# A language-model layer on one core: the first unit's q, k and v projection worked between token tiles 7 and 13

## The chip, the cores and the metric

The kernel runs on 1 core of one Trainium2 chip. The metric is the device time of one execution in microseconds (us), median over runs.

## The reference

The input is 2 sequences of 1024 token numbers, 2048 tokens in all, with rows of 512 features. The layer has three parts.

```
h   = where(is_hot[id], hot_emb[tok2hot[id]], cold_emb[tok2cold[id]] @ proj_w.T)   # 8000 hot rows of 512, 24000 cold of 128
h  += (softmax(causal(q @ k.T / sqrt(32))) @ v) @ w_out.T     # q, k, v = layernorm(h) @ w_project.T; 16 heads of 32
h  += routed top-2-of-16 experts (silu(x Wg) * (x Wu)) Wd, renormalised, + one shared expert    # x = layernorm(h)
```

## The kernel before

The program runs in stages, one instruction stream per engine, written out by hand and joined by semaphores alone. The order in a stream is the order in the code.

**Tables.** Two tables over all 32000 token numbers are built from the list of hot ids with one-hot matmuls into PSUM bank 0.

**Look-ups.** 128 tokens are one tile, 16 tiles (NT) in all. For each tile, TensorE multiplies the one-hot rows of its tokens with the tables (L1605 to L1613, PSUM banks 4 and 5 in turn), and VectorE picks the wanted column with two fused operations (`look_up`, L1523). After every four tiles `row_numbers` (L1535) turns the sums into row numbers for the gathers. All 16 look-ups come first.

**Token tiles.** For each tile c, GpSimd issues two indirect DMAs, one gathers cold rows (L1419) and one hot rows (L1423); then it takes the inverse standard deviation (`inv_std`, L691) of tile c - LAG - 1, with LAG = 4. TensorE turns the cold rows, multiplies them with the projection (L1631), and turns the normalised rows of tile c - 3 (L1639). ScalarE copies both results out of PSUM (L1460, L1464 into xnT). VectorE adds hot and cold rows and takes the statistics (`embed`, L1548), and one tile later it normalises (`norm`, L1559). SyncE stores each tile of h to HBM (L1370).

**The first projection.** Attention works on 8 units, one for 4 heads of one sequence. A unit needs its q, k and v projections: six pieces (FILLS) through PSUM bank 7, numbered q 0 and 1, k 2 and 3, v 4 and 5, where an even piece covers tokens 0 to 511 of the sequence, so tiles 0 to 3, and an odd one tiles 4 to 7. Units 2 to 8 have theirs worked inside the unit before. The first unit's six pieces go in TensorE's turns 11 to 16 of the tile loop (FILL0 = 11, L1642), one each turn, in the order 0 to 5. q and k are needed as a high part (float32r) and a low part. ScalarE copies the q pieces to the buffer `full` and VectorE the k pieces (`fill_evac`, L455); GpSimd makes from it the high part and then the low part (`split_part`, L427), in its own tile loop.

**Stacks.** `stack` (L394) spreads the two parts over the partitions with 16 DMAs of 128 KB for q and 16 for k, all issued by SyncE. q's come between the stores of h tiles 12 and 13, k's after the last store. The first scores (`first_scores`, L556) wait for all 32, for xnT of all 16 tiles (L1647) and for the v pieces.

**After that** come the 8 units of attention, the output projection and the expert stage; the change doesn't touch them.

Of the kernel before, what the change touches and what calls it, by code (L numbers as in the profile page):

```python
# [11 lines left out]
F32 = mybir.dt.float32  # L12
# [28 lines left out]
LAG = 4  # L41
# [3 lines left out]
FILL0 = NT // BATCH + 3  # L45
# [18 lines left out]
def build(nc, a, out):  # L64
    ctx = ExitStack()
    with ctx:
# [38 lines left out]
        oh_lo = tk("oh_lo", [HOT_P, HOT_C, 256], BF16)  # L105
        row_over_chunk = tk("row_over_chunk", [HOT_P, HOT_C])
# [31 lines left out]
        tk("stack_room", [P, HOT_C * 256 - HOT_C * 2], BF16)  # L138
# [255 lines left out]
        def stack(sp, u, b, sides=(0, 1), first=False):  # L394

            if not first:

                sp.wait_ge(s_S, HEAD + (u - 1) * STEPS)
            for side in sides:
                st = (q_stack, k_stack)[side][b]  # L400

                sp.wait_ge(s_lo, HEAD + 4 * u + 2 * side + 2)
                for r in range(4):
                    low = r % 2 if side == 0 else r // 2
                    src = part_lo if low else part_hi
                    for h in range(GH):
                        sp.dma_start(st[32 * r:32 * r + 32, h, :].bitcast(F32),
                                     src[32 * h:32 * h + 32, side, :].bitcast(F32)).then_inc(s_stack[b], 16)

        def att_sp(sp):  # L410
# [10 lines left out]
            group(GROUPS - 1, True)  # L421

# [54 lines left out]

        def fill_piece(pe, u, b, f, k, loads):

            if k == 0:  # L480

                pe.wait_ge(s_w, loads)
                copied, count = ((s_fdve, 0), (s_fact, 1), (s_fact, 2), (s_fdve, 1), (s_fdve, 2), (s_fact, 3))[f]
                pe.wait_ge(copied, HEAD + 3 * u + count)
            if f < 4:
# [867 lines left out]
        def _(sp):  # L1353
# [14 lines left out]
            for c in range(NT):  # L1368
                sp.wait_ge(s_h, c + 1)
                sp.dma_start(h_dram[c * P:(c + 1) * P, :], hot_vec[c][:, :]).then_inc(s_hst, 16)  # L1370
                if c == NT - LAG:
                    stack(sp, 0, 0, (0,), first=True)
            stack(sp, 0, 0, (1,), first=True)
# [4 lines left out]
        def _(pool):  # L1378
            for s in (s_lo, s_hi):
                pool.sem_inc(s, HEAD)  # L1380
# [49 lines left out]
            for c in range(NT - LAG - 1, NT):  # L1430
                inv_std(pool, c)
                if c < NT - 1:

                    half = c - NT + LAG + 1
                    split_part(pool, 0, 0, half // 2, half % 2, None)
# [4 lines left out]
        def _(act):  # L1440
            for s in (s_E, s_Ca, s_fact, s_ZR):
                act.sem_inc(s, HEAD)
            act.wait_ge(s_const, 9)
# [11 lines left out]
            for c in range(NT + 3):  # L1455
# [10 lines left out]
                if 0 <= c - FILL0 < FILLS:  # L1466
                    fill_evac(act, "act", 0, c - FILL0, 0)
# [4 lines left out]
        def _(dve):  # L1472
            for s in (s_M, s_Cd, s_Zr, s_Z, s_AT, s_fdve):
                dve.sem_inc(s, HEAD)
            step = Chain(dve, s_dve)
# [47 lines left out]
            def look_up(c):  # L1523
# [6 lines left out]
                for part, test, total in ((0, ALU.is_le, below), (1, ALU.is_equal, hot_no)):  # L1530
                    dve.scalar_tensor_tensor(out=prod[:, s, part, :], in0=iota_bf[:, :], scalar=tok_lo[:, c:c + 1],
                                             in1=bank(4 + s)[:, 256 * part:256 * part + 256], op0=test,
# [34 lines left out]
            for k in range(BATCHES):  # L1567
                for c in range(k * PER, (k + 1) * PER):
                    look_up(c)
                row_numbers(k)  # L1570
            for c in range(NT + 1):
                if c < NT:
# [3 lines left out]
                if 0 <= c + 1 - FILL0 < FILLS:  # L1576
                    fill_evac(dve, "dve", 0, c + 1 - FILL0, 0)
# [4 lines left out]
        def _(pe):  # L1582
# [22 lines left out]
            for c in range(NT):  # L1605
                if c >= 2:
                    pe.wait_ge(s_looked, 2 * (c - 1))
                b = bank(4 + c % 2)
# [4 lines left out]
                          skip_group_check=True).then_inc(s_look, 1)  # L1613
            pe.wait_ge(s_proj, 16)
            for c in range(NT + 3):
# [7 lines left out]
                if 1 <= c <= NT:  # L1623
                    t = c - 1
                    pe.wait_ge(s_coldC, t + 1)
                    if t == 1:

                        pe.wait_ge(s_looked, 2 * NT)
# [13 lines left out]
                if 0 <= c - FILL0 < FILLS:  # L1642

                    pe.wait_ge(s_xC, NT // BATCH)
                    for k in range(KC):
                        fill_piece(pe, 0, 0, c - FILL0, k, 16)
# [52 lines left out]
```

## Time and profile before

| | us |
|---|---|
| runs of the kernel before | 1059.1, 1061.99, 1067.91 (median 1061.99) |
| profiled execution, its own time | 1064.05 |
| its span | 1062.3 |
| TensorE busy in the span | 970.4 (91%) |
| VectorE, ScalarE, GpSimd busy | 555.0, 487.5, 299.4 |
| the chain that ended last: TensorE's share | 71% |

In the profile PE is TensorE's matmul, PEld its weight load, DVE is VectorE, ACT ScalarE, POOL GpSimd, SP SyncE; a q behind a name means the DMA instructions that the engine issues. Times in the rows are us from the start of the span.

### The profile page before, as it was taken

What the parts mean: (1) busy time and instruction counts of PE and PEld (TensorE: products, weight loads), DVE (VectorE), ACT (ScalarE), POOL (GpSimd) and SP (SyncE); (2) the same over time, 40 slices, a digit from 0 to 9 for tenths busy, and PEclk for the clock granted to TensorE, in tenths of its full rate; (3) what the DMA queues carried; (4) which work ended last, traced back from release to release, by engine and by line L of the source; (5) the groups of instructions that cost most, each with busy time, mean ns of one, the idle gap of its engine ahead of it and who ended that gap; (6) DMA issues with size and microseconds to landing.
All of it is one profiled execution on the core that took longest, in us unless ns stands there. A gap on an engine that the chain in (4) does not pass through costs nothing.

```text
span 1062.3 us, 20312 instructions
## 1 busy us (share of the span) xinstructions
PE 970.4 (91%) x6623; PEld 650.5 (61%) x6623; DVE 555.0 (52%) x1652; ACT 487.5 (46%) x1163; POOL 299.4 (28%) x320
## 2 busy tenths in 40 slices
PE   6668699999999999999998899899899999799994
PEld 5333468686776868686776687778644444344441
DVE  8875257575666657565667677578511111111110
ACT  7212177777767777777778422211122222222221
POOL 2276120111102020111111046333323643354432
PEclk9689899999999999999999999899999999999997
DMA  6133733250624334240533111711368757955443
GB/s 210 39 94 91 171 81 87 73 111 1 136 56 89 72 81 97 69 105 6 131 124 103 62 70 58 277 51 40 109 206 271 146 86 216 286 96 103 88 70 40
DMA packets 44564, 114.31 MB, mean 108 GB/s; under 512 B 9332, under 2 KB 11380, under 8 KB 42162
## 3 DMA queue, kind: packets, MB, share of 16 engines
q1 hardware_dynamic: 32146, 87.14, 28.7%
q0 software_dynamic: 12320, 25.90, 12.9%
q8 instruction: 57, 0.93, 0.4%
q14 instruction: 41, 0.34, 0.1%
HBM read 53.03 MB, written 25.17 MB: 74 GB/s over the span
## 4 chain that ended last, share of the span: by engine, by line
PE 71%; DVE 7%; issue 7%; DMA 6%; POOL 4%; ACT 3%; SPq 1%; POOLq 0%; ACTq 0%; DVEq 0%
PE psum L1258 11%; PE psum L518 11%; PE psum L488 8%; PE psum L531 7%; PE psum L508 7%; DMA w_dn<-in_wd 6%; PE psum L1339 6%; PE psum L493 5%; PE psum L1202 4%; PE psum L1186 3%; PE psum L1279 2%; PE psum L534 2%; PE psum L1301 1%; POOL hot_all L1423 1%; DVE oh_lo L1498 1%
## 5 line engine op out<-in xcount | busy, mean ns | idle before, releaser
L642 DVE CUSTOM_DVE_ANT_0 psum<-psum,mask_row 128x128 f32<-128x128 f32 (+7 forms) x256 | 194.3, 762 | 58.1 <-PE psum L508 55.7
L600 ACT ACTIVATE probs<-psum,nmax 128x128 f32<-128x128 f32 (+7 forms) x256 | 190.4, 744 | 47.4 <-DVE nmax L642 42.7
L1258 PE MATMUL psum<-attnT,x_T 128*128 x376 | 177.5, 594 | 8.2 <-SPq L748 6.9
L518 PE MATMUL psum<-ident,probs 128*128 128x128 f32 x1152 | 173.9, 276 | 4.7 <-ACT probsT L585 3.2
L508 PE MATMUL psum<-k_stack,q_stack 128*128 128x512 f32 (+2 forms) x384 | 155.5, 460 | 16.9 <-issue 8.8
L518 PEld LDWEIGHTS psum<-ident,probs 128*128 128x128 f32 x1152 | 136.9, 141 | 37.0 <-issue 18.9
L1159 DVE COPY x_T<-psum 128x512 f32<-128x512 f32 x47 | 32.5, 691 | 223.8 <-PE psum L1301 223.8
L585 ACT COPY probsT<-psum 128x512 f32<-128x512 f32 (+3 forms) x256 | 129.1, 504 | 37.8 <-PE psum L518 33.0
L488 PE MATMUL psum<-xnT,w_unit 128*128 128x512 f32 x256 | 130.5, 599 | 0.2 <-ACT full L463 0.2
L435 POOL CAST part_hi<-full 128x512 fp32r<-128x512 f32 x32 | 19.6, 612 | 350.7 <-ACT full L463 246.0
L859 POOL DMA_INDIRECT out<-xnT,slot_out x47 | 74.5, 1584 | 150.9 <-DMA out<-xnT,slot_out 104.6
L1258 PEld LDWEIGHTS psum<-attnT,x_T 128*128 128x128 f32 x376 | 67.2, 190 | 77.0 <-issue 76.9
L508 PEld LDWEIGHTS psum<-k_stack,q_stack 128*128 128x128 f32 x384 | 69.0, 202 | 62.0 <-ACT probs L600 39.3
L1339 PE MATMUL psum<-w_dn,gated_T 128*128 x188 | 88.6, 593 | 1.0 <-ACT gated_T L912 1.0
L531 PE MATMUL psum<-probsT,v_unit 128*32 128x128 f32 x2304 | 76.6, 276 | 0.8 <-ACT probsT L585 0.8
L531 PEld LDWEIGHTS psum<-probsT,v_unit 128*32 128x32 f32 x2304 | 59.2, 110 | 27.0 <-ACT probsT L585 21.7
L657 DVE TENSOR_TENSOR attnT<-psum,z_rows 128x128 f32<-128x128 f32 x64 | 18.7, 292 | 107.5 <-ACT z_rows L607 107.5
L931 ACT ACTIVATE xnT<-psum,slot_w 128x512 f32<-128x512 f32 x47 | 32.3, 687 | 83.3 <-PE psum L1339 83.3
L493 PE MATMUL psum<-w_unit,xnT 128*128 128x128 f32 x512 | 66.7, 275 | 0.3 <-DVE full L467 0.3
L587 DVE COPY probsT<-psum 128x128 f32<-128x128 f32 (+3 forms) x128 | 62.3, 486 | 3.0 <-PE psum L518 1.0
L493 PEld LDWEIGHTS psum<-w_unit,xnT 128*128 128x128 f32 x512 | 61.7, 192 | 0.5 <-issue 0.5
L906 ACT ACTIVATE silu_g<-psum 128x256 f32<-128x256 f32 x63 | 24.1, 383 | 79.9 <-PE psum L1258 63.4
(223 smaller groups left out, 1405.8 us busy)
## 6 DMA issues: line engine op xcount, KB each, us to landing
attnT<-in_wgu SPq DMA_DIRECT2D x16, 1024.0 KB, 5.4
q_stack<-part_hi SPq DMA_DIRECT2D x64, 128.0 KB, 2.4
q_stack<-part_lo SPq DMA_DIRECT2D x64, 128.0 KB, 2.4
k_stack<-part_hi SPq DMA_DIRECT2D x64, 128.0 KB, 2.4
k_stack<-part_lo SPq DMA_DIRECT2D x64, 128.0 KB, 2.4
w_dn<-in_wd SPq DMA_DIRECT2D x16, 512.0 KB, 6.1
out<-acc SPq DMA_DIRECT2D x17, 256.0 KB, 2.3
hot_all<-xn SPq DMA_DIRECT2D x4, 1024.0 KB, 8.0
```

The costliest lines, as they stand in the source:

```text
L488: mm = pe.matmul(bank(7), w_unit[:, k, side * P:(side + 1) * P], xnT[:, k, t0:t0 + 512], start=(k == 0), stop=(k == KC - 1), skip_group_ch ...
L493: mm = pe.matmul(bank(7)[:, k * P:(k + 1) * P], xnT[:, c, t0:t0 + P], w_unit[:, c, 2 * P:3 * P], start=(c == 0), stop=(c == KC - 1))
L508: mm = pe.matmul(dst[:, c0:c1], qs, k_stack[b][:, h, c0:c1], start=True, stop=True)
L518: mm = pe.transpose(bank(4 + m % 2)[:, (j - 4 * k) * P:(j - 4 * k + 1) * P], probs[n % PSLOTS][:, j * P:(j + 1) * P], ident[:, :])
L531: pe.matmul(bank(6)[32 * h:32 * h + 32, 0:P], v_unit[b][:, j, 32 * h:32 * h + 32], probsT[i % 2][:, h, j * P:(j + 1) * P], start=(j == 0), ...
L585: eng.copy(dst, src).then_inc(s_Ca, 1)
L587: eng.tensor_copy(dst, src).then_inc(s_Cd, 1)
L600: act.activation(probs[n % PSLOTS][:, 0:(i + 1) * P], bank(2 * (n % 2), 2)[:, 0:(i + 1) * P], ACT.Exp, bias=nmax[:, n % 4:n % 4 + 1], scal ...
L642: dve.tensor_tensor_reduce(out=row, in0=row, in1=mask_row[:, (QT - 1 - i) * P:QT * P], scale=1.0, scalar=3.0e38, op0=ALU.add, op1=ALU.min, ...
L859: pool.indirect_dma_start(out=out, out_offset=bass.IndirectOffsetOnAxis(ap=slot_out[:, j:j + 1], axis=0), in_=y_rows[j % ROUTED_RING], in_ ...
L1258: mm = pe.matmul(bank(2 + p), lhs(k), rhs(k), start=(k == 0), stop=(k == KC - 1), skip_group_check=True)
L1339: mm = pe.matmul(bank(6 + p), gated_T[:, p, k * P:(k + 1) * P], w_dn[:, bass.ds(half, 1), k, :].rearrange("p o n -> p (o n)"), start=(k == 0),
```

## The change

Six things change, all of them before the first scores.

1. Ten look-ups (`EARLY_LOOKS`) come ahead of the tile loop on TensorE and VectorE; the other six are done in turns 1 to 6 of the loop, one each, with `row_numbers` for tiles 8 to 11 in turn 2 and for 12 to 15 in turn 6. The late odd look-ups use bank 7 (`look_bank`).
2. LAG goes from 4 to 2, so GpSimd takes `inv_std` of tile c - 3 behind the gathers of tile c.
3. The six pieces are worked in TensorE's turns 7, 8, 9, 11, 12 and 13 in the order 0, 2, 4, 1, 3, 5 (`FIRST_FILL`). Piece 0 waits for all look-ups.
4. ScalarE makes the high part straight from bank 7 (`first_high`) and VectorE the low part from bank 7 and the high part (`first_low`), ahead of that turn's `embed`. GpSimd has no part in it any more, and the copies to `full` go.
5. SyncE issues the q stacks behind the store of h tile 10. ScalarE issues the k stacks, 8 DMAs at the end of its turn 13 and 8 at the end of its turn 14.
6. ScalarE, VectorE and SyncE wait for the last store of h before attention. A block of unused room (`stack_room`) moves, so that the q and k stacks lie over memory that is free by then.

```diff
@@ -38,11 +38,12 @@
 WRING = 4
-LAG = 4
+LAG = 2
+EARLY_LOOKS = 10
+FIRST_FILL = {7: 0, 8: 2, 9: 4, 11: 1, 12: 3, 13: 5}
 SPLIT0 = 5
 SLOT0 = 6
-FILL0 = NT // BATCH + 3
 PSLOTS = 2
@@ -103,6 +104,7 @@
         oh_lo = tk("oh_lo", [HOT_P, HOT_C, 256], BF16)
+        tk("stack_room", [P, HOT_C * 256 - HOT_C * 2], BF16)
         row_over_chunk = tk("row_over_chunk", [HOT_P, HOT_C])
@@ -135,7 +137,6 @@
         projT = tk("projT", [LATENT, D])
-        tk("stack_room", [P, HOT_C * 256 - HOT_C * 2], BF16)
         hot_all = tk("hot_all", [P, NT, D])
@@ -391,7 +392,7 @@
-        def stack(sp, u, b, sides=(0, 1), first=False):
+        def stack(sp, u, b, sides=(0, 1), first=False, quarters=range(4)):
@@ -399,8 +400,8 @@
-                sp.wait_ge(s_lo, HEAD + 4 * u + 2 * side + 2)
-                for r in range(4):
+                sp.wait_ge(s_lo, HEAD + (3 + side if first else 4 * u + 2 * side + 2))
+                for r in quarters:
                     low = r % 2 if side == 0 else r // 2
@@ -419,6 +420,9 @@
             group(GROUPS - 1, True)
+        def look_bank(c):
+            return bank(4 if c % 2 == 0 else 5 if c < EARLY_LOOKS else 7)
@@ -475,6 +479,53 @@
+        def first_high(act, c):
+            f = FIRST_FILL[c]
+            n = list(FIRST_FILL.values()).index(f)
+            side, half = f // 2, f % 2
+            cols = slice(half * 512, half * 512 + 512)
+            act.wait_ge(s_fill, HEAD + n + 1)
+            if side == 0:
+                act.activation(part_hi[:, 0, cols], bank(7), ACT.Copy, scale=-ATT_SCALE).then_inc(s_hi, 1)
+            elif side == 1:
+                act.copy(part_hi[:, 1, cols], bank(7)).then_inc(s_hi, 1)
+            elif half == 0:
+                act.copy(v_unit[0][:, 0:4, :].rearrange("p a n -> p (a n)"), bank(7)).then_inc(s_fact, 1)
+        def first_low(dve, c):
+            f = FIRST_FILL[c]
+            n = list(FIRST_FILL.values()).index(f)
+            side, half = f // 2, f % 2
+            cols = slice(half * 512, half * 512 + 512)
+            if side < 2:
+                dve.wait_ge(s_hi, HEAD + 2 * half + side + 1)
+                if side == 0:
+                    dve.scalar_tensor_tensor(out=part_lo[:, 0, cols], in0=bank(7), scalar=-ATT_SCALE,
+                                             in1=part_hi[:, 0, cols].bitcast(F32), op0=ALU.mult,
+                                             op1=ALU.subtract).then_inc(s_lo, 1)
+                else:
+                    dve.tensor_tensor(part_lo[:, 1, cols], bank(7), part_hi[:, 1, cols].bitcast(F32),
+                                      ALU.subtract).then_inc(s_lo, 1)
+            elif half == 1:
+                dve.wait_ge(s_fill, HEAD + n + 1)
+                dve.tensor_copy(v_unit[0][:, 4:8, :].rearrange("p a n -> p (a n)"), bank(7)).then_inc(s_fdve, 1)
+        def first_piece(pe, c):
+            f = FIRST_FILL[c]
+            pe.wait_ge(s_w, 16)
+            pe.wait_ge(s_xC, 4 * (f % 2) + 4)
+            if f == 0:
+                pe.wait_ge(s_looked, 2 * NT)
+            elif f == 1:
+                pe.wait_ge(s_fact, HEAD + 3)
+            else:
+                pe.wait_ge(s_lo, HEAD + {2: 1, 4: 2, 3: 3, 5: 4}[f])
+            for k in range(KC):
+                fill_products(pe, 0, f, k)
         def fill_piece(pe, u, b, f, k, loads):
@@ -482,6 +533,10 @@
                 pe.wait_ge(copied, HEAD + 3 * u + count)
+            fill_products(pe, b, f, k)
+        def fill_products(pe, b, f, k):
             if f < 4:
@@ -1368,16 +1423,14 @@
                 sp.dma_start(h_dram[c * P:(c + 1) * P, :], hot_vec[c][:, :]).then_inc(s_hst, 16)
-                if c == NT - LAG:
+                if c == 10:
                     stack(sp, 0, 0, (0,), first=True)
-            stack(sp, 0, 0, (1,), first=True)
+            sp.wait_ge(s_hst, 16 * NT)
             att_sp(sp)
         def _(pool):
-            for s in (s_lo, s_hi):
-                pool.sem_inc(s, HEAD)
             pool.memset(xn[:, 0, :], 0.0).then_inc(s_zeros, 1)
@@ -1429,17 +1482,14 @@
                 inv_std(pool, c)
-                if c < NT - 1:
-                    half = c - NT + LAG + 1
-                    split_part(pool, 0, 0, half // 2, half % 2, None)
             att_pool(pool)
         def _(act):
-            for s in (s_E, s_Ca, s_fact, s_ZR):
+            for s in (s_E, s_Ca, s_fact, s_ZR, s_hi):
                 act.sem_inc(s, HEAD)
+            act.sem_inc(s_fact, 2)
             act.wait_ge(s_const, 9)
@@ -1463,15 +1513,19 @@
                              bank(2 + t % 2).rearrange("p (k n) -> p k n", k=KC)).then_inc(s_xC, 1)
-                if 0 <= c - FILL0 < FILLS:
-                    fill_evac(act, "act", 0, c - FILL0, 0)
+                if c in FIRST_FILL:
+                    first_high(act, c)
+                if c in (13, 14):
+                    stack(act, 0, 0, (1,), first=True, quarters=(2 * c - 26, 2 * c - 25))
+            act.wait_ge(s_hst, 16 * NT)
             att_act(act)
         def _(dve):
-            for s in (s_M, s_Cd, s_Zr, s_Z, s_AT, s_fdve):
+            for s in (s_M, s_Cd, s_Zr, s_Z, s_AT, s_fdve, s_lo):
                 dve.sem_inc(s, HEAD)
+            dve.sem_inc(s_fdve, 2)
             step = Chain(dve, s_dve)
@@ -1529,7 +1583,7 @@
                     dve.scalar_tensor_tensor(out=prod[:, s, part, :], in0=iota_bf[:, :], scalar=tok_lo[:, c:c + 1],
-                                             in1=bank(4 + s)[:, 256 * part:256 * part + 256], op0=test,
+                                             in1=look_bank(c)[:, 256 * part:256 * part + 256], op0=test,
                                              op1=ALU.mult, accum_out=total[:, c:c + 1]).then_inc(s_looked, 1)
@@ -1564,17 +1618,22 @@
-            for k in range(BATCHES):
-                for c in range(k * PER, (k + 1) * PER):
-                    look_up(c)
-                row_numbers(k)
+            for c in range(EARLY_LOOKS):
+                look_up(c)
+                if c % PER == PER - 1:
+                    row_numbers(c // PER)
             for c in range(NT + 1):
+                if c in FIRST_FILL:
+                    first_low(dve, c)
                 if c < NT:
                     norm(c - 1)
-                if 0 <= c + 1 - FILL0 < FILLS:
-                    fill_evac(dve, "dve", 0, c + 1 - FILL0, 0)
+                if 1 <= c <= NT - EARLY_LOOKS:
+                    look_up(EARLY_LOOKS + c - 1)
+                    if (EARLY_LOOKS + c) % PER == 0:
+                        row_numbers((EARLY_LOOKS + c) // PER - 1)
+            dve.wait_ge(s_hst, 16 * NT)
             att_dve(dve)
@@ -1602,15 +1661,18 @@
             pe.wait_ge(s_tohC, 2)
-            for c in range(NT):
+            def look(c):
                 if c >= 2:
                     pe.wait_ge(s_looked, 2 * (c - 1))
-                b = bank(4 + c % 2)
+                b = look_bank(c)
                 oh = tok_ohT[:, c, :]
                           skip_group_check=True).then_inc(s_look, 1)
+            for c in range(EARLY_LOOKS):
+                look(c)
             pe.wait_ge(s_proj, 16)
@@ -1625,7 +1687,7 @@
-                        pe.wait_ge(s_looked, 2 * NT)
+                        pe.wait_ge(s_looked, 2 * EARLY_LOOKS)
                     if t >= 2:
@@ -1639,11 +1701,10 @@
                     mm.then_inc(s_xT, 1)
-                if 0 <= c - FILL0 < FILLS:
-                    pe.wait_ge(s_xC, NT // BATCH)
-                    for k in range(KC):
-                        fill_piece(pe, 0, 0, c - FILL0, k, 16)
+                if 1 <= c <= NT - EARLY_LOOKS:
+                    look(EARLY_LOOKS + c - 1)
+                if c in FIRST_FILL:
+                    first_piece(pe, c)
             pe.wait_ge(s_xC, NT)
```

## Rows read from the trace of the kernel before

**Rows 1.** Windows by stage: stretch, length, busy PE, PEld, DVE, ACT, POOL; clock; DMA; GB/s.

```profile
37.40:61.00 23.60, 16.92 (x57) 6.48 (x58) 18.51 (x94) 0.74 (x3) 12.24 (x12) 0.56 0.13 20
...
88.00:128.30 40.30, 30.04 (x142) 18.66 (x143) 15.78 (x35) 7.21 (x15) 16.25 (x19) 0.93 0.62 148
...
187.00:660.00 473.00, 456.03 (x4377) 346.13 (x4377) 308.77 (x854) 321.56 (x778) 79.68 (x102) 0.99 0.32 80
```

**Rows 2.** Timeline of SyncE's DMA issues: start us, us, line, transfer, how many.

```profile
102.78 2.53 SPq L407 DMA_DIRECT2D q_stack<-part_hi  x4
...
113.86 1.56 SPq L1370 DMA_DIRECT2D h_scratch<-hot_all  x3
...
115.46 5.18 SPq L407 DMA_DIRECT2D k_stack<-part_hi  x8
...
120.69 5.04 SPq L407 DMA_DIRECT2D k_stack<-part_lo  x8
```

**Rows 3.** Windows, the same columns: while the k stacks are issued, and after.

```profile
115.46:125.70 10.24, 3.30 (x28) 2.82 (x27) 1.68 (x4) 1.17 (x2) 0.80 (x1) 0.87 1.00 244
...
125.70:128.30 2.60, 0.00 (x0) 0.00 (x1) 0.00 (x0) 0.00 (x0) 0.00 (x0) 0.50 0.54 106
```

**Rows 4.** Issues of line 407 over the run: duration ns min/median/max.

```profile
L407 SPq DMA_DIRECT2D k_stack<-part_lo x64: 590/592/1918, 120.7 to 532.4; - x64
```

**Rows 5.** Timeline: the last copy to xnT and the first scores.

```profile
119.60 0.58 ACT L1464 COPY xnT<-psum 128x512 f32<-128x512 f32 x1 [0.87 <-PE psum L1639]
...
128.33 0.77 PE L508 MATMUL psum<-k_stack,q_stack 128*128 128x256 f32 x2 [8.77 <-issue]
```

**Rows 6.** Timeline of GpSimd, the cold gathers of two tiles.

```profile
75.19 1.05 POOL L1419 DMA_INDIRECT cold_all<-in_cold_emb,cold_row  x1 [0.17 <-issue]
...
78.32 1.04 POOL L1419 DMA_INDIRECT cold_all<-in_cold_emb,cold_row  x1 [0.17 <-issue]
```

**Rows 7.** Timeline of VectorE, ScalarE and TensorE, one tile's turn.

```profile
75.57 0.68 DVE L1553 TENSOR_TENSOR hot_all<-hot_all,psum 128x512 f32<-128x512 f32 x1
...
77.22 0.15 DVE L1557 TENSOR_SCALAR mv<-mv 128x1 f32<-128x1 f32 x1
...
78.18 0.59 DVE L1564 TENSOR_SCALAR xn<-hot_all,mv,rstd 128x512 f32<-128x512 f32 x1 [0.81 <-POOL rstd L695]
...
76.88 0.27 ACT L1460 COPY cold_T<-psum 128x128 f32<-128x128 f32 x1
...
75.70 0.66 PE L1639 MATMUL psum<-ident,xn 128*128 128x128 f32 x4 [1.51 <-DVE xn L1564]
```

**Rows 8.** Timeline of VectorE: look-ups 4 and 8, and the end of 9.

```profile
43.07 0.48 DVE L1531 SCALAR_TENSOR_TENSOR prod<-iota_bf,tok_lo,psum 128x256 f32<-128x256 bf16 x1
...
47.86 0.48 DVE L1531 SCALAR_TENSOR_TENSOR prod<-iota_bf,tok_lo,psum 128x256 f32<-128x256 bf16 x1
...
49.07 0.48 DVE L1531 SCALAR_TENSOR_TENSOR prod<-iota_bf,tok_lo,psum 128x256 f32<-128x256 bf16 x1
```

**Rows 9.** Timeline of TensorE: the first, the second and the last piece.

```profile
88.69 3.60 PE L488 MATMUL psum<-xnT,w_unit 128*128 128x512 f32 x8
...
93.54 3.60 PE L488 MATMUL psum<-xnT,w_unit 128*128 128x512 f32 x8
...
113.93 3.74 PE L493 MATMUL psum<-w_unit,xnT 128*128 128x128 f32 x32
```

**Rows 10.** Timeline: copies of a piece and its low part on GpSimd.

```profile
92.33 0.60 ACT L463 ACTIVATE full<-psum 128x512 f32<-128x512 f32 x1 [2.85 <-PE psum L488]
...
102.46 0.69 DVE L467 COPY full<-psum 128x512 f32<-128x512 f32 x1 [2.02 <-PE psum L488]
...
106.78 1.26 POOL L437 TENSOR_TENSOR part_lo<-full,part_hi 128x512 fp32r<-128x512 f32 x1
```

**Rows 11.** Timeline of TensorE: the projection of tile 0 and of a later one.

```profile
55.88 2.08 PE L1631 MATMUL psum<-projT,cold_T 128*128 128x512 f32 x2
...
76.31 1.02 PE L1631 MATMUL psum<-projT,cold_T 128*128 128x512 f32 x2
```


## The prediction

> **What bounds the kernel now.** I read the windows by stage first. From 187 to 660 us TensorE is busy 456.0 of 473.0 us at a granted clock of 0.99: attention is TensorE's, and nothing in the change touches its instructions. From 88 to 128.3 us TensorE is busy 30.0 of 40.3 us, VectorE 15.8 and ScalarE 7.2 [rows 1]: this stage waits, and only here can the change act. So the question is one number: when do the first scores start? They start at 128.33 us, and the last copy to xnT had ended at 120.18 [rows 5]. Between them lies SyncE's queue. It issues the 16 q stacks from 102.78 on and the last three stores of h behind them, at 113.86. The 16 k stacks then go from 115.46 to 125.73, and 2.6 us later the last has landed and scores start [rows 2, 5]. The k stacks are thus what ends last, with the last token tiles 8 us ahead of them. Behind the start everything shifts with it, as a TensorE-bound queue of fixed work: 1 us here is 1 us of the total.
>
> **Part 1: look-ups inside the loop.** The first eight look-ups are untouched, so the first eight tiles' gathers can start when they did. VectorE is done with the tenth at 49.55 [rows 8]. The first embed needs the gathers of tiles 0 and 1, so I put it at 51.5 (49.6 if they are early, 54 if late). One turn costs VectorE 1.80 us for embed (75.57 to 77.37) and 0.59 for norm [rows 7]. Four look-ups with their row numbers take 4.79 (43.07 to 47.86), and one look-up 0.80 (half of 47.86 to 49.47) [rows 8]: the six that moved, with two sets of row numbers, take 2 x 4.79 - 2 x 0.80 = 8.0. Up to the last look-up in turn 6 that is 7 embeds, 6 norms and 8.0 us without the last row numbers (1.6): 12.6 + 3.5 + 6.4 = 22.5, and 0.1 a turn for hops. So piece 0, which waits for all look-ups, starts near 51.5 + 22.5 + 0.7 = 74.7. GpSimd's own pace, 78.32 - 75.19 = 3.13 a tile [rows 6], is a little faster than VectorE's turn of 3.3; it no longer sets the pace. Piece 0 starts 14 us sooner than the 88.69 of before [rows 9].
>
> **Part 2: six pieces in turns 7 to 13.** Before, the first and the last of six successive pieces start 113.93 - 88.69 = 25.24 apart, 5.05 a turn [rows 9]. Now a piece holds bank 7 until ScalarE has the high part (taken as 0.60) and VectorE the low part (taken as its copy, 0.69: same size, same bank) [rows 10], 1.4 us with hops, while TensorE has 1.25 us of other work between pieces (92.29 to 93.54 [rows 9]). So 5.1 a turn; GpSimd's pass (1.26 for a low part) goes. If the low part with its two sources took GpSimd's 1.26 instead, four pieces would cost 2.3 more. Turns 7, 8, 9: two steps, 10.2. From 9 to 11 lies a turn without a piece, which costs VectorE's 2.5: 7.6. Turns 11, 12, 13: 10.2. The last piece starts at 102.7 and ends at 106.5 (3.74 long) against 117.67 before: 11 us gained at this point.
>
> **Part 3: q stacks.** Their 16 issues wait for the low part of piece 1, near 97, and end near 107, beside tile work. No one waits for them; the stores of tiles 11 to 13 sit behind, as tiles 13 to 15 did before. The last store goes when tile 15 is embedded and is no longer queued. At no cost, as long as it lands before xnT is full; with the 2.6 us of the k stacks it does.
>
> **Part 4: k stacks on ScalarE, the deciding one.** The profile before has no DMA issue on ScalarE. The nearest row is SyncE's: 5.04 for 8, so 0.63 each [rows 2], the median being 0.59 in all units and the longest 1.92 [rows 4]. Bounds: 0 (the engine hands them over) and 1.92 each. I take 0.63, the same transfer through the same kind of issue. What is queued behind them on ScalarE matters: 8 issues stand at the end of turn 13, after its wait for piece 5. Behind these are tile 14's cold_T copy and tile 11's xnT copy (0.27 and 0.58 [rows 5, 7]), then 8 more issues, then tile 15's cold_T copy. TensorE's projection of tile 15 waits for that, VectorE's embed for TensorE, and so on to xnT. Sum: 106.7 + 5.0 + 0.9 + 5.0 = 117.6. The tail behind it: cold_T 0.27, projection 1.02 [rows 11], embed 1.80, two norms 1.18, turning 0.66 [rows 7], xnT copy 0.58, hops 0.4, together 5.9: 123.5. TensorE is nearly idle from 107 to then. In the stretch from 37.4 to 61 its granted clock was 0.56 [rows 1] and a projection took 2.08 instead of 1.02 [rows 11]; at the low level (1.2 GHz) the tail takes 1.5 more: 125.0. The k stacks land at 117.6 + 2.6 = 120.2, tile 15's store near 123: both earlier. So tiles end last now, held up by ScalarE's issues. The first scores meet a low clock as they did before (0.50 ahead of them [rows 3]), so nothing is added for that.
>
> **The sum.** 125.0 against 128.3 is 3.3 us earlier; I take 3. The profiled execution took 1064.05 us, 2 us above the median of 1061.99, so it would read 1061, and the median comes to 1059.
>
> **A rule against it.** During the k stacks the DMA share was 1.00 at 244 GB/s [rows 3]. At that rate their 2 MB take 8.6 us whoever issues them. The Trainium skill says the same in "DMA: Bandwidth & Descriptors", section "Issuing engines are not separate DMA queues": DMAs of all engines run on the same 16 DMA engines, and issuing from several saves only the sequencer's time, usually small beside the transfer. By that rule ScalarE would hardly be held and the total would be rival A's; the rows, 0.63 us an issue, don't call it small.
>
> **Rivals.**
> - **A, issues on ScalarE are cheap.** At 0.3 us or less the block costs at most 5 instead of 10 us and the tail ends near 118 to 120. The transfers bound it: 106.7 + 8.6 + 2.6 = 117.9. That is 10.4 earlier at most: 1051.6 to 1055. For it: three stores of h, twice the size each, took 1.56 us to issue, 0.52 each [rows 2], so the time isn't the bytes'. Against it: 0.59 is the median over all units. Chance 0.25.
> - **B, slower: each issue costs ScalarE more than SyncE.** The place is the same block. Break-even is 0.63 + 3.3/16 = 0.84 us each. At 1.2 the block is 9 us longer, scores start at 134 and the total is 1068. For it: ScalarE would hold q's last transfers and the stores in the same DMA engines, and single issues took up to 1.92. Against it: only three stores overlap. Chance 0.2.
> - **C, the early turns lose what the order wins.** If VectorE's turns 0 to 6 take 4 instead of 3.3 us, waiting for gathers or for GpSimd, piece 0 starts at 79 and scores at 129: 1062 to 1064, no difference. Against it: gathers run at 3.13 us a tile. Chance 0.15.
>
> **How the numbers follow.** My forecast (gain of 0 to 6 us) has 0.4. The range takes in A nearly to its bound and B to 1.2 us an issue: 1051 to 1068; beyond lie 1 in 10 for a gain at A's bound with the run-to-run spread (1059 to 1068 among three runs), and 1 in 10 for B's far part. 1% is 10.6 us, about what a measurement of this kernel can tell from no change. A gain of that size needs all of A and a little more: 0.08. A loss of it needs issues of 1.5 us: 0.05. The rest, 0.87, is within 1%.
>
> **What the changed profile would show.** Piece 0 near 75 and piece 5 near 103 on TensorE; if piece 0 is at 79 or later, part 1 is wrong. Steps of 5.1 between pieces in adjacent turns; 6 or more would say that VectorE's low part holds bank 7. ScalarE's two blocks of 8 issues with 5 us each: 2 or less is A, 9 or more is B. First scores right behind the last copy to xnT, no longer behind a landing stack. The time from first scores to the end unchanged, near 934 us; if it moves by more than 3 us, the premise that attention only shifts is wrong.

## The result, and the profile after

The changed kernel takes 1066.99 us (median of 20 runs, 1060.34 to 1070.23), the kernel before 1063.45 (20 runs, 1059.1 to 1068.71). The ratio is 1.0029 [1.0015, 1.0043]: about 3.1 us slower, where I had forecast 3 us faster. The number stayed inside the range; the sign was wrong.

The profiled execution of the changed kernel took 1067.77 us, its span is 1066.0. Its look-ups, pieces and stacks, in the order of the prediction's steps. In the timeline the columns are start, length, engine, line, operation, tiles, and in brackets the engine's idle time before it and what ended it. First TensorE's pieces: they answer to [rows 9].

```profile
75.34 5.37 PE L543 MATMUL psum<-xnT,w_unit 128*128 128x512 f32 x8 [3.40 <-DVE prod L1585]
...
82.22 3.67 PE L543 MATMUL psum<-xnT,w_unit 128*128 128x512 f32 x8
...
105.31 3.81 PE L548 MATMUL psum<-w_unit,xnT 128*128 128x128 f32 x32
```

Piece 0 starts 13.3 us sooner than the 88.69 of before, but takes 5.37 us instead of 3.60. TensorE had idled 3.40 us for the last look-up (L1585), and its first matmuls ran at the low clock (0.68 granted over the 5.37 us; 1.00 is the level of 2.4 GHz, 0.50 that of 1.2). The last piece ends at 109.1 instead of 117.67. Next the DMA issues of SyncE and of ScalarE, which answer to [rows 2, 4]:

```profile
100.03 3.38 SPq L408 DMA_DIRECT2D q_stack<-part_hi  x4
103.46 2.49 SPq L408 DMA_DIRECT2D q_stack<-part_lo  x4
105.99 2.79 SPq L408 DMA_DIRECT2D q_stack<-part_hi  x4
108.83 2.67 SPq L408 DMA_DIRECT2D q_stack<-part_lo  x4
111.53 13.80 SPq L1425 DMA_DIRECT2D h_scratch<-hot_all  x5
...
109.16 8.22 ACTq L408 DMA_DIRECT2D k_stack<-part_hi  x8
117.48 0.27 ACT L1510 COPY cold_T<-psum 128x128 f32<-128x128 f32 x1 [11.63 <-issue]
117.53 0.52 ACTq L408 DMA_DIRECT2D k_stack<-part_lo  x1
117.64 0.59 ACT L1514 COPY xnT<-psum 128x512 f32<-128x512 f32 x1
118.07 4.65 ACTq L408 DMA_DIRECT2D k_stack<-part_lo  x7
122.81 0.27 ACT L1510 COPY cold_T<-psum 128x128 f32<-128x128 f32 x1 [4.58 <-issue]
```

This is where the time went. ScalarE's first block of 8 issues takes 8.22 us, its second 5.17 (0.52 + 4.65). Between them ScalarE turns once to its copies, and cold_T of tile 14 (L1510) comes out of PSUM after 11.63 us without work. For the first 3.3 of these ScalarE waits for piece 5; for the rest nothing else in the profile keeps it (the "issue" named there), it is handing over DMAs. SyncE's queue is not idle beside this block: the last of its q issues end at 111.5, and three of the five stores in its last row, of 256 KB each, are issued from 111.53 to 114.91; they land 5.0 to 5.8 us later. The same line's durations, one issue each (ns, min/median/max):

```profile
L408 ACTq DMA_DIRECT2D k_stack<-part_hi x8: 595/948/1831, 109.2 to 116.8; - x8
L408 ACTq DMA_DIRECT2D k_stack<-part_lo x8: 515/612/791, 117.5 to 122.1; - x8
```

The windows (length, busy time of PE, PEld, DVE, ACT and POOL, clock, DMA share, GB/s) during the two blocks, behind them, and of attention. They answer to [rows 1, 3]:

```profile
109.16:117.40 8.24, 1.48 (x8) 0.71 (x6) 2.88 (x6) 0.00 (x0) 0.80 (x1) 0.79 0.98 251
117.53:122.80 5.27, 2.93 (x6) 1.39 (x6) 2.19 (x5) 0.70 (x2) 0.80 (x1) 0.70 0.94 245
122.80:129.40 6.60, 4.06 (x14) 2.46 (x14) 2.74 (x6) 2.51 (x5) 0.80 (x1) 0.60 0.31 107
...
187.00:660.00 473.00, 454.54 (x4366) 344.89 (x4366) 307.70 (x852) 320.85 (x777) 78.78 (x100) 0.99 0.32 81
```

In the first block TensorE works 1.48 of 8.24 us, VectorE 2.88 and ScalarE nothing, while the DMA engines are busy at 0.98. The tail follows on TensorE and ScalarE, answering to [rows 5, 11]:

```profile
117.80 2.07 PE L1693 MATMUL psum<-projT,cold_T 128*128 128x512 f32 x2 [7.16 <-ACT cold_T L1510]
...
128.79 0.59 ACT L1514 COPY xnT<-psum 128x512 f32<-128x512 f32 x1 [0.40 <-PE psum L1701]
...
129.43 0.80 PE L563 MATMUL psum<-k_stack,q_stack 128*128 128x256 f32 x2 [0.68 <-ACT xnT L1514]
```

The scores wait for the last copy to xnT (L1514) and no longer for a landing stack: what ends last did change place, as forecast. But they start at 129.43, after the 128.33 of before, not at 125.0.

### The profile page after: what moved, and what is told of

The parts are those of the page before. It is cut to its first block, busy times and chain, and to the rows that moved or that the text cites. A ratio compares the mean times of both kernels' runs of the same rounds, so it can differ in the third digit from the quotient of the medians.

```text
span 1066.0 us, 20302 instructions
## 1 busy us (share of the span) xinstructions
PE 973.5 (91%) x6623; PEld 650.8 (61%) x6623; DVE 556.6 (52%) x1654; ACT 488.7 (46%) x1165; POOL 293.4 (28%) x312
## 4 chain that ended last, share of the span: by engine, by line
PE 73%; DVE 9%; DMA 7%; issue 4%; ACT 3%; ACTq 1%; SPq 1%; POOL 0%; POOLq 0%; DVEq 0%
PE psum L1313 11%; PE psum L573 11%; PE psum L543 10%; PE psum L563 7%; PE psum L586 7%; DMA w_dn<-in_wd 6%; PE psum L1394 5%; PE psum L548 5%; PE psum L1257 5%; PE psum L1241 3%; PE psum L1334 2%; PE psum L589 2%; PE psum L1356 1%; ACTq L408 1%; DVE oh_lo L1552 1%
## 5 line engine op out<-in xcount | busy, mean ns | idle before, releaser
L439 POOL CAST part_hi<-full 128x512 fp32r<-128x512 f32 x28 | 17.2, 613 | 341.0 <-ACT full L467 236.6
```

## The experiments

**Theory:** ScalarE's issues cost more than SyncE's 0.63 us because the q stacks and the stores of h, handed over by SyncE, fill the same DMA engines, and ScalarE's queue, being in order, holds the last two tiles' copies meanwhile. **Rival 1:** an issue on ScalarE is dearer in itself. **Rival 2:** the late first piece makes the loss. A third question, why the time is 3 us longer when the start is only 1.1 us later, came up with the result. All edits but the last three are to the changed kernel. The microseconds in brackets behind a ratio are its distance from 1 times 1063.

**All k stacks on SyncE.**

```diff
+                if c == 12:
+                    stack(sp, 0, 0, (1,), first=True)
             sp.wait_ge(s_hst, 16 * NT)
...
-                if c in (13, 14):
-                    stack(act, 0, 0, (1,), first=True, quarters=(2 * c - 26, 2 * c - 25))
```

> All 16 k stacks are issued by SyncE, behind its store of h tile 12; ScalarE issues none. My theory (ScalarE's two blocks of issues hold the last tiles): the projections of tiles 14 and 15 no longer wait for a cold_T copy, xnT is full near 119 us instead of 129.4, SyncE issues k from about 112 to 123 and the last three stores behind it, and the first scores start near 126, the softmax near 127. So about 3 us earlier than the changed kernel. Rival (the last tiles are slow by themselves, at TensorE's low clock and in VectorE's turns): xnT is full at 125 or later although ScalarE is free, and nothing is gained.

Measured: 1063.23 us, ratio 0.9982 [0.9966, 0.9999] (-1.9 us), so about 5 us better than the changed kernel (3.6 against its repeat further down, 1.0016). Its timeline on SyncE, ScalarE and TensorE:

```profile
112.35 4.98 SPq L408 DMA_DIRECT2D k_stack<-part_hi  x8
117.37 5.03 SPq L408 DMA_DIRECT2D k_stack<-part_lo  x8
122.44 1.58 SPq L1425 DMA_DIRECT2D h_scratch<-hot_all  x3
...
119.02 0.58 ACT L1516 COPY xnT<-psum 128x512 f32<-128x512 f32 x1 [0.40 <-PE psum L1701]
...
125.20 0.77 PE L563 MATMUL psum<-k_stack,q_stack 128*128 128x256 f32 x2 [6.22 <-issue]
```

Without issues on ScalarE the last copy to xnT comes at 119.02 instead of 128.79. The tiles are 9.8 us earlier, and the stacks end last again: scores start at 125.20. So ScalarE's issues were the hold.

**The q stacks behind the last store of h.**

```diff
-                if c == 10:
+                if c == NT - 1:
                     stack(sp, 0, 0, (0,), first=True)
```

> SyncE issues the q stacks behind the last store of h instead of behind tile 10's, so ScalarE's k issues meet only the stores of tiles 11 and 12. Theory (an issue on ScalarE costs 0.63 us and the first block took 8.2 us because the DMA engines were full with q): the first block takes 5.0 to 5.5 us and the second about 5. Rival (issues on ScalarE cost about 1 us in themselves, at least at first): the first block takes 8 again. In either case the q stacks end last: issued from about 122 to 132, first scores at 133 to 137, the whole 4 to 7 us longer than the changed kernel.

This takes the q transfers away from beside ScalarE's first block, and with them two of the three stores of h that had been held up behind them; the q stacks then end last themselves, so the whole is slower: 1071.98 us, 1.0061 [1.0039, 1.0084], first scores at 135.54. What it was for is the block:

```profile
109.15 5.43 ACTq L408 DMA_DIRECT2D k_stack<-part_hi  x8
...
114.73 0.51 ACTq L408 DMA_DIRECT2D k_stack<-part_lo  x1
...
115.27 4.64 ACTq L408 DMA_DIRECT2D k_stack<-part_lo  x7
```

The same 8 issues from the same engine at the same moment take 5.43 us here and 8.22 in the changed kernel (8.16 in its repeat, 8.50 with 16 look-ups ahead, below). The price on ScalarE is SyncE's, 0.64 to 0.68 each; the rest, 2.8 us, is the other queue's load, q stacks and stores together. Rival 1 falls. That the two engines hinder each other in the act of issuing, and not by their transfers, doesn't fit the longest issue: it ran from 114.90 to 116.73, when SyncE had issued its last store (until 114.91) and the DMA share was still 0.98.

**The first k block ahead of the wait for piece 5.**

```diff
+                if c == 13:
+                    stack(act, 0, 0, (1,), first=True, quarters=(0, 1))
                 if c in FIRST_FILL:
                     first_high(act, c)
-                if c in (13, 14):
-                    stack(act, 0, 0, (1,), first=True, quarters=(2 * c - 26, 2 * c - 25))
+                if c == 14:
+                    stack(act, 0, 0, (1,), first=True, quarters=(2, 3))
```

> ScalarE issues the first 8 k stacks ahead of its wait for piece 5 in turn 13, not behind it; the data are ready near 104.5 and ScalarE stood idle from 105.9 to 109.1. If ScalarE's hold sets the end: the block starts near 105.9 and, beside q all the way, takes 8 to 9 us; cold_T of tile 14 is copied near 114.5 instead of 117.5, and the first scores start near 126.5 instead of 129.4, 3 us earlier. If instead the bytes set the end (q, k and stores in one set of DMA engines, full either way), the two blocks stretch by as much as they start earlier and the scores stay at 129.

1065.21 us, 1.0010 [0.9989, 1.0032], first scores at 127.17. The blocks are "105.81 6.18" and, in the second, 0.62 and 6.73 us: the first starts 3.35 us sooner and stands beside q's issues all the way, for which I had expected 8 to 9 us; it takes less than before. The second grows from 5.17 to 7.35, and beside it are no q issues after 112.91, but the four stores of h behind them, issued from 112.96 to 116.67. So the stores bunched behind q weigh at least as much as q itself. Of 3.35 us ahead 2.3 arrive. How much a load lengthens a block is not fixed: with q beside it, the first block takes 6.33, 7.47 and 7.91 us in three profiles further down whose code up to there is the same.

**All 16 look-ups ahead.**

```diff
-EARLY_LOOKS = 10
+EARLY_LOOKS = 16
...
-            return bank(4 if c % 2 == 0 else 5 if c < EARLY_LOOKS else 7)
+            return bank(4 if c % 2 == 0 else 5)
```

> All 16 look-ups come ahead of the tile loop again, the rest of the change stays. Theory: the first piece took 5.37 us instead of 3.60 because TensorE stood idle for 3.4 us ahead of it, waiting for the last look-ups, and its clock fell; without this wait it takes 3.6. VectorE starts its first embed 5 us later, GpSimd loses as much at its first inverse deviation, so piece 0 starts at 74 to 76, as in the changed kernel, and the first scores come 1 to 2 us earlier than 129.4. Rival: TensorE has so little to do in turns 0 to 6 that the piece meets the low clock anyway (5.4 us), or the later start costs more than the look-ups in the loop do, and scores start at 130 or later.

1065.58 us, 0.9997 [0.9979, 1.0015] (-0.3), first scores at 127.26. Its first piece, and its first block:

```profile
75.01 3.60 PE L543 MATMUL psum<-xnT,w_unit 128*128 128x512 f32 x8
...
107.05 8.50 ACTq L408 DMA_DIRECT2D k_stack<-part_hi  x8
```

Piece 0 starts at the same time (75.01 against 75.34) with no idle time ahead of it, and takes 3.60 us. So the six look-ups inside the loop bring no earlier start and cost 1.8 us at the low clock (3.0 in the repeat below, where piece 0 takes 6.62). That is rival 2's true part: about 2 of the lost microseconds.

**The changed kernel once more, unchanged.**

> The changed kernel once more, unaltered. The part ahead of the first scores should repeat (129.4, within 0.7 us). For the rest, two theories. Scatter: in the profiled runs so far the time from the first scores to the end was 934.0 before, 936.6 changed and 936.1, 934.9, 931.6 and 938.9 in four variants that are alike in that part; the granted clock falls or not in TensorE's short pauses, above all in the 2.1 us ahead of the output projection. Then this run gives any value from 931 to 939. Fixed: the shifted start itself costs 2.6 us later on; then it gives 936.6 again, within 0.5. The ratio should be between 1.001 and 1.005.

1066.14 us, 1.0016 [0.9997, 1.0034], first block "109.62 8.16", first scores at 129.82. The block and the start repeat. The time points the same way as in the result, but here the interval takes in 1. The rest, from the first scores to the end, is 935.0 and not 936.6: scatter, not a fixed cost of 2.6.

**k stacks shared between the queues.** High parts on ScalarE ahead of the wait in turn 13, low parts on SyncE behind the store of tile 12.

```diff
+                if c == 12:
+                    stack(sp, 0, 0, (1,), first=True, quarters=(2, 3))
...
+                if c == 13:
+                    stack(act, 0, 0, (1,), first=True, quarters=(0, 1))
                 if c in FIRST_FILL:
                     first_high(act, c)
-                if c in (13, 14):
-                    stack(act, 0, 0, (1,), first=True, quarters=(2 * c - 26, 2 * c - 25))
```

> ScalarE issues the 8 high k stacks ahead of its wait for piece 5 in turn 13, and SyncE the 8 low ones behind its store of tile 12; nothing else is altered. If the hold of ScalarE is the whole loss, and the DMA engines bound what is left: ScalarE's block from 105.8 to 112, SyncE's k block from about 114 to 119, the last stores to 120.5 and landed by 123; first scores near 122, 7 us earlier than the changed kernel and 6 earlier than before; ratio near 0.995. If the last tiles need ScalarE earlier than that, or 4 MB of stacks and 1.3 MB of stores keep the DMA engines busy until 124, scores start at 125 as in the run with all k on SyncE.

1061.03 us, 0.9973 [0.9956, 0.9991] (-2.9), first scores at 124.23, where I had expected 122. The tiles are done (last copy to xnT at 119.98), and SyncE's k issues end at 119.51 as forecast, but the last transfers take another 4.7 us, with the DMA share at 1.03 from 119.51 to 124.20: the bytes bound the end, as the rival said. It starts 1.0 us sooner than with all k on SyncE; by the times the two can't be told apart (0.9973 and 0.9982, their intervals overlap).

**The same with all 16 look-ups ahead.** The two edits of the last experiment and the fourth together.

> The same split of the k stacks, and all 16 look-ups ahead of the tile loop. The run with 16 look-ups had the first piece in 3.60 us instead of 5.37 and everything behind it 2.1 us earlier. If this adds up: first scores near 120, 8 us earlier than before, median near 1056 to 1058, ratio 0.993. If the DMA engines bound it, the 2 us are lost again and it equals the run with ten look-ups.

1059.3 us, 0.9960 [0.9944, 0.9975] (-4.3), first scores at 121.32:

```profile
103.31 7.91 ACTq L408 DMA_DIRECT2D k_stack<-part_hi  x8
...
113.61 5.22 SPq L408 DMA_DIRECT2D k_stack<-part_lo  x8
118.87 1.57 SPq L1425 DMA_DIRECT2D h_scratch<-hot_all  x3
...
120.36 0.59 ACT L1516 COPY xnT<-psum 128x512 f32<-128x512 f32 x1 [0.40 <-PE psum L1703]
...
121.32 0.77 PE L563 MATMUL psum<-k_stack,q_stack 128*128 128x256 f32 x2 [1.00 <-ACT xnT L1516]
...
123.87 0.58 PE L563 MATMUL psum<-k_stack,q_stack 128*128 128x256 f32 x1 [1.78 <-ACT probs L655]
```

Tiles and stacks now end within 1 us of each other. The scores start 8.1 us sooner than in the changed kernel and the time falls by 7.3 us by the ratio in the result (0.0069 of 1063), by 6.0 against its repeat (0.0056). All k on SyncE with 16 look-ups ahead was not run, so how much of this the sharing brings is open. One microsecond more is lost right behind: the second scores come 2.55 us after the first (1.68 in the repeat of the changed kernel), since ScalarE and VectorE wait for the last stores of h, issued at 118.87, before the softmax.

**Dummy matmuls against the low clock.** To the last kernel, 19 matmuls of 128x512 whose result is not used: 2 in each of turns 14 to 18, 4 ahead of the last wait for xnT, 5 ahead of the output projection.

```diff
+            def keep_warm(n):
+                for _ in range(n):
+                    pe.matmul(bank(4), ident[:, :], xnT[:, 0, 0:512], start=True, stop=True)
...
+                if c >= 14:
+                    keep_warm(2)
+            keep_warm(4)
             pe.wait_ge(s_xC, NT)
             att_pe(pe)
+            keep_warm(5)
             moe_pe(pe)
```

> The kernel with the split k stacks and 16 look-ups ahead, and 19 more matmuls whose result no one reads: two in each of TensorE's turns 14 to 18, four ahead of its wait for the full xnT, five ahead of the output projection, where it pauses for 2.1 us. Theory (the idle time lets the clock fall, and the first work behind it pays): the granted clock stays near 1.00 in both places, the first units' pieces take 1.02 a pair instead of 1.92, the output projection's first matmuls are 0.23 us apart and not 0.43, and the time from first scores to end is 2 to 4 us shorter than in the kernel without them, near 931. Rival: the matmuls delay the last tiles' turns by about what they win (19 x 0.43 = 8 us of them, some on the path), and the total is the same or longer.

1060.35 us, 0.9964 [0.9948, 0.998]. No better. The granted clock is 1.00 from 107 to 125 us (without them 0.72 up to 119 and 0.68 behind it), but the dummies stand on the path: "119.55 5.32 x12" reaches to the first scores, 124.30, while the last copy to xnT began at 119.75. The scores start 3.0 us later than without them and the time is 1.1 longer; the rest of this profile is 932.6 us, with the clock at 1.00 in 595 to 615 and 0.95 in 640 to 672. Whether the five dummies ahead of the output projection win this is not shown, since the rest scatters from 931.6 to 939.1.

**Fewer of them:** 1 in each of turns 14 to 18, none at the end, 2 ahead of the output projection.

```diff
+                if c >= 14:
+                    keep_warm(1)
             pe.wait_ge(s_xC, NT)
             att_pe(pe)
+            keep_warm(2)
             moe_pe(pe)
```

> e5_split16 with one dummy matmul (128x512, result unused) in each of turns 14 to 18 and two ahead of the output projection, none at the end of the attention work. If the part of the time that scatters is TensorE's granted clock falling in short pauses: first scores at 121.3 as in e5_split16, the clock at 1.00 through the output projection (the first matmuls 0.23 apart), some 933 us from the first scores to the end of the span, 1056 to 1058 us in all, ratio to the kernel before 0.993 to 0.995. Rival: the dummies stand on the path, or the clock falls elsewhere instead: ratio 0.996 or more.

1058.98 us (6 runs), 0.9951 [0.9933, 0.9969] (-5.2): with e5_split16 the best, and not to be told from it. Its timeline on SyncE, ScalarE and TensorE, and its windows at the tail, the output projection and behind it:

```profile
113.04 5.69 SPq L408 DMA_DIRECT2D k_stack<-part_lo  x8
...
118.78 0.59 ACT L1516 COPY xnT<-psum 128x512 f32<-128x512 f32 x1 [0.71 <-PE psum L1707]
...
121.19 0.47 PE L563 MATMUL psum<-k_stack,q_stack 128*128 128x256 f32 x2 [1.58 <-issue]
```

```profile
107.00:119.00 12.00, 9.40 (x38) 4.66 (x37) 7.73 (x17) 2.90 (x7) 2.41 (x3) 1.00 1.01 259
...
595.00:615.00 20.00, 19.57 (x99) 15.97 (x99) 14.98 (x33) 5.05 (x9) 4.18 (x5) 1.00 0.32 120
640.00:672.00 32.00, 28.39 (x159) 24.45 (x158) 19.33 (x67) 5.89 (x12) 15.63 (x22) 0.89 0.28 101
```

The clock in the tail is 1.00 and xnT is complete 1.6 us earlier, but the scores start where they did: now the k stacks, issued until 118.73, end last. The clock won at the output projection (1.00 instead of 0.91 in 595 to 615) is lost again in the next pause: 0.89 instead of 0.95 in 640 to 672.

**The kernel before with two dummy matmuls ahead of the output projection.**

```diff
             att_pe(pe)
+            for _ in range(2):
+                pe.matmul(bank(4), ident[:, :], xnT[:, 0, 0:512], start=True, stop=True)
             moe_pe(pe)
```

> The kernel before with two dummy matmuls (results unused) in TensorE's pause ahead of the output projection, nothing else. If that pause decides on the clock of the output projection: first scores at 128.3 as before, the output projection's first matmuls 0.23 apart, 0.5 to 1.5 us gained on the median since only some executions lose the clock there, ratio about 0.999. Rival: no difference, or the pause moves behind the dummies: ratio 1.000 or a little above.

1062.53 us, 0.9999 [0.9984, 1.0013] (12 and 17 runs). No difference. The clock is 1.00 in 595 to 615 and 0.89 in 640 to 672; the first profile of before had 1.00 and 0.96 there without dummies. The surprise stands in the part that I had not touched: first scores at 126.08, not at 128.33. In this timeline of TensorE the first projections, then piece 0:

```profile
55.87 1.69 PE L1631 MATMUL psum<-projT,cold_T 128*128 128x512 f32 x2
57.51 1.02 PE L1631 MATMUL psum<-projT,cold_T 128*128 128x512 f32 x2
...
86.57 3.60 PE L488 MATMUL psum<-xnT,w_unit 128*128 128x512 f32 x8
```

In the first profile of before the projections took 2.08 [rows 11], 1.14, 1.10 and 1.58 us, and piece 0 came at 88.69. So the start that I had taken as fixed goes with TensorE's clock in the first turns: 0.63 from 64 to 68 us in the first profile of before, 1.00 here.

**The kernel before, unchanged, twice more.**

> The kernel before, unchanged, one more profiled execution. Open is why the changed kernel's first scores come only 1.1 us later than in the first profile of before while its time is 3.1 us longer. In e10_before_warm, which has the same code up to the scores, they came at 126.08 and not at 128.33: tiles 1 to 3 had their projections at the full clock (1.02 instead of 1.1 to 1.6 us). If the first profile of before had a late start, this one shows first scores near 126 and piece 0 near 86.6, and the changed kernel (129.4, 129.8) is 3 to 4 us later. Rival: 128.3 is the usual start; then they come near 128.3 here too and e10_before_warm was the odd one.

> As e11_before_again, once more: first scores near 126 if the late start of the first profile was the exception, near 128.3 if it is the rule. The time from the first scores to the end of the span between 931 and 939 as in all others.

One execution each: first scores at 126.48 (span 1060.1) and at 128.31 (span 1062.1). From the first, and from the second:

```profile
87.15 3.60 PE L488 MATMUL psum<-xnT,w_unit 128*128 128x512 f32 x8
```

```profile
87.64 3.60 PE L488 MATMUL psum<-xnT,w_unit 128*128 128x512 f32 x8
```

Neither expectation holds alone: both starts are usual. The clock is one source of the difference, not the only one. In the second, piece 0 comes only 1.1 us later than in the kernel with two dummies, the scores 2.2 later; the other 1.1 goes with SyncE's queue, where one q issue takes 2.44 us (the longest of the kernel with two dummies takes 1.33, the median 0.59). It lies in this row:

```profile
106.84 4.36 SPq L407 DMA_DIRECT2D q_stack<-part_hi  x4
```

Over four profiles of the same code up to the scores they are 128.33, 126.08, 126.48 and 128.31, mean 127.3; the changed kernel's are 129.43 and 129.82, mean 129.6. It starts 2.3 us later, not 1.1. From the first scores to the end the four take 933.6 to 934.8 us (mean 934.1), the two 936.6 and 935.0 (mean 935.8).

## Why the prediction was wrong

| kernel | first scores | ratio to before [95%] |
|---|---|---|
| before (four profiles) | 126.1 to 128.3 | 1 |
| changed (two profiles) | 129.4, 129.8 | 1.0029 [1.0015, 1.0043]; repeat 1.0016 |
| q stacks last | 135.5 | 1.0061 |
| first k block ahead | 127.2 | 1.0010 |
| 16 look-ups ahead | 127.3 | 0.9997 |
| k stacks on SyncE | 125.2 | 0.9982 |
| k shared, 10 look-ups ahead | 124.2 | 0.9973 |
| k shared, 16 look-ups ahead | 121.3 | 0.9960 |
| the same, 19 dummies | 124.3 | 0.9964 |
| the same, 7 dummies | 121.2 | 0.9951 |

**What bounds it: right.** The one number was the start of the first scores: the later it is, the longer the time, within what the ratios can tell (intervals of 0.0014 to 0.0023 to either side). Two lines differ in size: the q stacks' 6 us cost 3.4 to 5 (by the ratios, or by the medians), and the 19 dummies' 3.0 us cost 1. Windows 187 to 660 are the same work at the same clock.

**Part 1: right.** First embed at 52.41 (51.5 forecast), piece 0 at 75.34 (74.7). Rival C is out. What I missed is what stood ahead of piece 0: six look-ups that wait on VectorE leave TensorE idle 3.40 us, and then the piece runs at the low clock. I had put that at nothing here and charged it only to the tail.

**Part 2: steps right, first size wrong.** Behind the first, which takes 6.88 us to the next, the pieces come 5.1 to 5.2 us apart in adjacent turns and 7.67 across the turn without one; the low part on VectorE takes 0.69 (L505, L509). Piece 0's 5.37 instead of 3.60 adds 1.8, and the last piece ends at 109.1 instead of 106.5.

**Part 3: wrong.** "At no cost" looked only at who waits for the q stacks. No one does, but their 16 issues, forecast from 97 to 107 and so just done as ScalarE's block begins, run from 100.03 to 111.50, and the three stores behind them to 114.91, beside the block from 109.16 on. The q-last experiment prices both together at 2.8 us.

**Part 4 is the step that failed:** 0.63 us an issue, "two blocks of 5.0". The place, the queue behind it and what ends last are as forecast. The size is 8.22 + 5.17 = 13.39 for 16, so 0.84 us each: the break-even of rival B to the digit. By that alone the start would have been unchanged, 128.4; with piece 0 it is later. The price of 0.63 came from a queue that fed the DMA engines alone, behind its own three stores. My own row showed them full (1.00) then; I should have asked what a second queue pays when they already are. From the prediction's 125.0 to 129.4: piece 0 and hops +2.5, first block +3.2, second +0.2, the copies between the blocks -0.8 (0.15 instead of 0.9, as an issue doesn't wait for the copy to end), the tail -0.7 (6.7 instead of 7.4). Sum 4.4.

**The base: wrong by 1 us.** 128.33 was one draw of 126.1 to 128.3. Against the mean of four the forecast would have been 2.3 us faster, not 3.3, and the result is 2.3 slower.

**"Unchanged, near 934": right within its bound of 3 us.** The changed kernel's two are 1.7 above the mean of before, which takes in one profile with two dummies in this part. All variants scatter from 931.6 to 939.1, so these 1.7 us have no cause shown. Where the single profiles differ is TensorE's clock behind short pauses. For the output projection, the changed kernel:

```profile
602.03 0.76 PE L1257 MATMUL psum<-wo_hi,at_hi 128*128 128x512 f32 x1 [2.15 <-DVE at_lo L1062]
602.59 0.63 PE L1257 MATMUL psum<-wo_hi,at_lo 128*128 128x512 f32 x1
603.02 0.63 PE L1257 MATMUL psum<-wo_lo,at_hi 128*128 128x512 f32 x1
```

After the same pause of 2.15 us the first profile of before starts these matmuls 0.23 us apart, this one 0.43; that is 1.6 us of the 2.6 between the two profiles. But the later repeats of before had the low clock there as well (0.86 in 600 to 612), so it is no mark of the change. Which executions lose the clock, and why, stays open.

**Rival B** had the right mechanism and sign, with a chance of 0.2. **Rival A** is out. It goes with the Trainium skill's "DMA: Bandwidth & Descriptors", section "Issuing engines are not separate DMA queues", which says two things. That DMAs of all engines run on the same 16 DMA engines agrees with ScalarE's block beside SyncE's q stacks and stores: 8.22 against 5.43 us. That the issue is usually small beside the transfer doesn't hold here: 8 issues that meet no q stacks still hold ScalarE for 5.43 us. From the first I had worked out how long the k bytes take; that q's bytes and the stores run on the same engines at the same time spoke against the change, and I left it to rival B.

## What to carry to other kernels

An issue's duration read from a queue that runs alone is a lower bound for a second queue: look at what the first queue will be moving in the stretch in which the second will issue, its held-up stores too, and ask what compute stands behind the issues on that engine. Before a forecast of a few microseconds, ask whether the start it is measured against is the same in every execution; one profile cannot tell. When several waits meet at one point, shorten them together: with all k stacks on ScalarE the tiles ended last, with all on SyncE the stacks did, 6.2 us behind the tiles; shared, and with 16 look-ups ahead, both end within 1 us.

## What the runs showed of the hardware that I had not expected

- A DMA issue (32 partitions, 128 KB) took 0.59 to 0.68 us on SyncE or ScalarE alike when one queue ran, and on ScalarE a median of 0.95, at most 1.83, while SyncE's transfers ran beside it (DMA share 0.98). A full share alone doesn't make issues long: SyncE's 16 k issues took 10.05 us at 0.99 when no other engine issued. Single long issues also occur on SyncE's queue alone (1.49 us in the first profile of before, 2.44 in its last).
- ScalarE hands over DMAs while its last copy still runs: cold_T's copy began at 117.48, the next issue at 117.53.
- TensorE's clock behind a pause of 2.15 us differed from execution to execution (1.00 or 0.86 in 600 to 612), worth 1.6 us. With two dummies in that pause it was 1.00 there, but 0.89 and not 0.95 to 0.99 in 640 to 672 in both profiles with them, and nothing was won on the kernel before: 0.9999 [0.9984, 1.0013]. With five it stayed at 0.95 there.
